# Three queues for the edge transfers, and a second staging buffer in the sort, in a graph kernel

## The chip, the cores and the metric

The kernel runs on one core of a Trainium2 chip. The metric is the device time of one execution in microseconds. Three executions of the kernel before took 7155.8, 7169.51 and 7184.21 us (median 7169.51). A fourth was profiled and took 7184.49 us, of which 7182.9 us are the span from its first to its last instruction.

## The reference

There are 3125 nodes with 64 features and 100,000 edges, given as `src` and `dst`, sorted by `dst`. Four graph networks follow one another; behind each the result is added to `x` and normalised.

1. Five layers, each of
```
h = leaky(x @ W1 + b1) @ W2 + b2
e = leaky(edge_attr_32 @ We1 + be1) @ We2 + be2
x = layernorm(x + res_w * segment_sum(h[src] * e * dot_scale, dst)) * ln_g + ln_b
```
2. A graph convolution with weights by degree.
3. Two transformer convolutions, with a softmax over the edges of each node.
4. `x + (x + segment_sum(relu(x[src] + edge_attr_64), dst))`, then the last normalisation.

Only 1 and 4 read edge attributes edge by edge. In 2 and 3 the kernel uses a matrix of edge counts between all pairs of nodes.

## The kernel before, in words

The five engines run programs of their own that are tied by semaphores. The stages are separated by barriers.

**Sort.** The edges are put into a new order, by blocks of 256 source nodes and 128 target nodes. They are laid out as 125 partitions by 800 columns, and one step (`t`, `j`) treats 8 columns, 1000 edges; there are 100 steps. SyncE loads, broadcast to all partitions, the keys and the block numbers of the step's edges (`load_keys`, lines 614 to 618, two steps ahead) and its 32-wide attributes (`load_attr`, three steps ahead). VectorE compares the keys (`find_slots`, from line 1579) to find the place of each edge. TensorE computes `e` for the five layers, which depends on nothing in the layers, and ScalarE copies it from PSUM into `stage`, a ring of four slots whose rows hold 64 floats of `edge_attr_64`, 5 x 64 floats of `e`, and 2 ids. The 64-wide attributes are loaded into the slot by a DMA that ScalarE issues (`load_stage`, line 900), behind a wait on `rows_sent`: the slot has to be free of the rows of four steps ago. GpSimd waits for that load (`stage_loaded`, line 788) and for ScalarE's last copy (`stage_ready`), and sends the rows to their places in HBM with eight indirect DMAs a step (line 792). When ScalarE's copies of the last step are done, VectorE computes tables (from line 1605), and the barrier follows.

**Unpack.** 144 groups of 8 tiles of 128 edges. For each group 8 small DMAs load the ids (`load_ids`, line 550), TensorE and VectorE count, and one-hot matrices are stored to HBM (`ohsD`).

**Edge passes.** One for each of the five layers and one for network 4. A pass has 72 pairs of groups. For a pair, SyncE loads its one-hot matrices (`load_hots`, line 688) and all three DMA-issuing engines load its 16 tiles of edge rows (`load_edges`, line 548), each engine the share of every 8 tiles that line 456 gives it. They may start on pair i when VectorE has made the messages of pair i-4 (`m_ready`). Once in four pairs an engine first reads the addresses of its tiles into registers (`starts`, line 539). ScalarE besides makes four copies of table slices a pair (`slice_tables`, line 1004). TensorE gathers the rows of pair i (line 1287, 96 matmuls) between the scatters of pair i-3 (line 1296, 48 matmuls). VectorE runs four operations a pair: the message (line 1790, in the last pass 1792), the two subtractions that split it into three bf16 parts (1804, 1810), and the one-hot of the targets (1682).

**Between** the fifth and the sixth pass lie network 2 and the two convolutions of 3, which the change doesn't touch.

Of the kernel before, what the change touches and what calls it, by code (L numbers as in the profile page):

```python
# [17 lines left out]
U16 = mybir.dt.uint16  # L18
# [6 lines left out]
D = 64  # L25
# [7 lines left out]
EP = 125  # L33
ET = E // EP
# [18 lines left out]
JB = 4  # L53
IB = ET // JB
CC = 20
NCHUNK = IB // CC
CS = 8
SR = 4
# [9 lines left out]
KEYS = [(a, min(a + P, ET)) for a in range(0, ET, P)]  # L68
# [31 lines left out]
def graph_kernel(nc, x_in, src_in, dst_in, a32_in, a64_in, w1_in, b1_in, w2_in, b2_in, we1_in, be1_in,  # L100
                 we2_in, be2_in, resw_in, dots_in, lng_in, lnb_in, gw_in, gb_in, conv_in, out):
    with ExitStack() as ctx:
# [3 lines left out]
        def sem(name):  # L106
            return ctx.enter_context(nc.semaphore(name))

        def dram(name, shape, dt=F32):
            return nc.dram_tensor(name, shape, dt, kind="Internal").ap()  # L110


        rows = dram("rows", (ROWS, ROW))
        keyT = dram("keyT", (ET, EP))
        blkT = dram("blkT", (ET, EP), BF16)
        ohsD = dram("ohsD", (NG, P, 2 * GT * P), U8)
        maskD = dram("maskD", (W, P, NP))
# [31 lines left out]
        def carver(at=0):  # L149

            at = [at]

            def carve(*shape, dt=F32):
                n = 1
                for s in shape:
                    n *= s
                words = -(-n * {F32: 4, I32: 4, U32: 4, BF16: 2, U16: 2, U8: 1}[dt] // 4)
                v = big[:, at[0]:at[0] + words]
                at[0] += words
                assert at[0] <= BIG, (at[0], BIG)  # L160
                if dt != F32:
                    v = v.bitcast(dt)
                if len(shape) == 2:
                    v = v.rearrange("p (a b) -> p a b", a=shape[0])
                if len(shape) == 3:
                    v = v.rearrange("p (a b c) -> p a b c", a=shape[0], b=shape[1])
                return v
            carve.at = at
            return carve


        carve = carver()
# [20 lines left out]
        ohv = [carve(JB * CC, 32, dt=BF16) for _ in range(2)]  # L193
        ohw = [carve(JB * CC, W + 1, dt=BF16) for _ in range(2)]
        carve = carver(shared)
        keyb = carve(2, CS * EP)
        blkb = carve(2, CS * EP, dt=BF16)
        lhot = carve(2, CS * EP + 4, dt=BF16)
        tabh = carve(IB + 1, 2, W, dt=BF16)
        keyS = carve(len(KEYS), EP)  # L200
        blkS = carve(len(KEYS), EP + 1, dt=BF16)
        stage = carve(SR, CS, ROW)
        attr = carve(SR, CS, DA)
        sidx = carve(SR, CS, dt=U32)
        late = carve.at[0]
        slotf = carve(ET)
# [42 lines left out]
        carve = carver(b_base)  # L249
# [17 lines left out]
        carve = carver()  # L267
# [19 lines left out]
        carve = carver(c_base)  # L287
# [8 lines left out]
        carve = carver(c_base)  # L296
# [19 lines left out]
        def bank(b, n=1):  # L316
            return ps[:, b * 512:(b + n) * 512]

        pacc = bank(0, 4)
        pA, pB, pC, pD = bank(4), bank(5), bank(6), bank(7)  # L320
# [13 lines left out]
        key_kept = sem("key_kept")  # L334
        key_stored = sem("key_stored")
# [8 lines left out]
        ranked = sem("ranked")  # L344
        slot_ready = sem("slot_ready")
        slot_chain = sem("slot_chain")
        stage_loaded = [sem(f"stage_loaded{r}") for r in range(SR)]
        attr_loaded = [sem(f"attr_loaded{r}") for r in range(SR)]
        edge_weights = sem("edge_weights")
        be2_chain = sem("be2_chain")  # L350
        be2_ready = sem("be2_ready")
        attr_turned = sem("attr_turned")
        attr_kept = sem("attr_kept")
        e_up = sem("e_up")
        e_biased = sem("e_biased")
        e_act = sem("e_act")
# [96 lines left out]

        PE, DVE, SP = mybir.EngineType.PE, mybir.EngineType.DVE, mybir.EngineType.SP
        POOL, SCALAR = mybir.EngineType.Pool, mybir.EngineType.Activation
        SP_SHARE, POOL_SHARE, ACT_SHARE = (0, 4), (4, 7), (7, 8)
        SOFT = 16 * (POOL_SHARE[1] - POOL_SHARE[0])
        HARD = 16 * GT - SOFT
        CLAMPED = "the table was clamped when it was made on the chip"
# [1 line left out]
        def hold(eng):  # L461

            eng.nop(nofuse=True)
# [64 lines left out]
        def past(i, k):  # L528

            return not isinstance(i, int) or i >= k  # L530

        def chunk(t, j, k):

            return t + (j + k) // JB, (j + k) % JB
# [47 lines left out]
        def _(sp):  # L582
            sp.dma_start(src_i[0:EP, :], src_in.rearrange("(p t) -> p t", p=EP)).then_inc(ids_loaded, 16)
            sp.dma_start(dst_i[0:EP, :], dst_in.rearrange("(p t) -> p t", p=EP)).then_inc(ids_loaded, 16)
            a32_v = a32_in.rearrange("(p t) f -> p t f", p=EP)

            def load_attr(t, j):
                tiles = bass.ds(j * IB + t * CS, CS)
                sp.dma_start(attr[0:EP, j, :, :], a32_v[:, tiles, :]).then_inc(attr_loaded[j], 16)
# [14 lines left out]
            sp.dma_start(be2r[0:3, :], be2_in.rearrange("(o l) f -> o (l f)", o=1).to_broadcast([3, LAYERS * D])).then_inc(edge_weights, 16)  # L604
            for k, (a, b) in enumerate(KEYS):
                sp.wait_ge(key_kept, 2 * k + 2)
                sp.dma_start(keyT[a:b, :], keyS[0:b - a, k, :]).then_inc(key_stored, 16)
                sp.dma_start(blkT[a:b, :], blkS[0:b - a, k, 0:EP]).then_inc(key_stored, 16)
            sp.wait_ge(key_stored, 32 * len(KEYS))
            sp.wait_ge(counted, NCHUNK)  # L610
# [3 lines left out]
            def load_keys(t, j):  # L614
                r = j % 2
                own = bass.ds(j * QT + t, 1)
                sp.dma_start(keyb[0:EP, r, :], keyT_v[own, :].to_broadcast([EP, CS * EP])).then_inc(key_loaded[r], 16)
                sp.dma_start(blkb[:, r, :], blkT_v[own, :].to_broadcast([P, CS * EP])).then_inc(key_loaded[r], 16)

            load_keys(0, 0)  # L620
            load_keys(0, 1)

            def feed(t, j):
                i = t * JB + j
                if not past(i, QN - 2):
                    sp.wait_ge(ranked, i + 1)
                    hold(sp)
                    load_keys(*chunk(t, j, 2))
                if past(i, 1) and not past(i, QN - 3):
                    sp.wait_ge(attr_kept, i)  # L630
                    hold(sp)
                    load_attr(*chunk(t, j, 3))

            def feed_more(t, j):
                i = t * JB + j
                sp.wait_ge(ranked, i + 1)
                hold(sp)
                load_keys(*chunk(t, j, 2))
                sp.wait_ge(attr_kept, i)
                hold(sp)  # L640
                load_attr(*chunk(t, j, 3))

            for j in range(JB):
                feed(0, j)
# [117 lines left out]
        def _(pool):  # L762
# [22 lines left out]

            with pool.Fori(0, QT) as t:
                for j in range(JB):
                    pool.wait_ge(stage_loaded[j], t * 16 + 16)
                    pool.wait_ge(stage_ready, t * JB + (j + 1))
                    hold(pool)  # L790
                    for c in range(CS):
                        pool.indirect_dma_start(  # L792
                            out=rows[:, :], out_offset=bass.IndirectOffsetOnAxis(ap=sidx[0:EP, j, c:c + 1], axis=0),
                            in_=stage[0:EP, j, c, :], in_offset=None).then_inc(rows_sent[j], 16)
# [67 lines left out]
        def _(act):  # L862
            for k, (a, b) in enumerate(KEYS):
                act.wait_ge(key_turned, 2 * k + 1)
                act.copy(keyS[0:b - a, k, :], pC[0:b - a, 0:EP]).then_inc(key_kept, 1)
                act.wait_ge(key_turned, 2 * k + 2)
                act.copy(blkS[0:b - a, k, 0:EP], pD[0:b - a, 0:EP]).then_inc(key_kept, 1)
            for s in range(NCHUNK):
# [6 lines left out]
            def bias(t, j, p):  # L875
                at = (t * JB + j) * 3 + p
                n = P if p < 2 else D
                act.wait_ge(e_up, at + 1)
                if past(at, 2):
                    act.wait_ge(e_act, at - 1)  # L880
                act.activation(hb[0:n, (j + p) % 2, :, :], ups[0:n, :, 0:2 * EP], ACT.Identity, bias=be1[0:n, p:p + 1]).then_inc(e_biased, 1)  # L881
# [10 lines left out]
            def stage_ids(t, j):  # L892
                tiles = bass.ds(j * IB + t * CS, CS)
                act.wait_ge(slot_ready, t * JB + (j + 1))
                act.copy(sidx[0:EP, j, :], slotf[0:EP, tiles])
                act.copy(stage[0:EP, j, :, IDS:ROW], ids[0:EP, tiles, :]).then_inc(stage_ready, 1)

            a64_v = a64_in.rearrange("(p t) f -> p t f", p=EP)

            def load_stage(t, j):  # L900
                act.dma_start(stage[0:EP, j, :, 0:D], a64_v[:, bass.ds(j * IB + t * CS, CS), :]).then_inc(stage_loaded[j], 16)

            def keep_attr(t, j):
                i = t * JB + j
# [5 lines left out]
            def fill(t, j, last_one=False):  # L910
                i = t * JB + j
                bias(t, j, 0)
                if past(i, 1):
                    keep_edges(*chunk(t, j, -1), 4)
                    stage_ids(*chunk(t, j, -1))
                bias(t, j, 1)
                if past(i, JB):
                    act.wait_ge(rows_sent[j], t * (16 * CS))
                    hold(act)
                load_stage(t, j)  # L920
                keep_edges(t, j, 0)
                keep_edges(t, j, 1)
                bias(t, j, 2)
                if not last_one:
                    keep_attr(*chunk(t, j, 1))
                keep_edges(t, j, 2)
                keep_edges(t, j, 3)

            keep_attr(0, 0)
            for j in range(JB):  # L930
                fill(0, j)
# [1086 lines left out]
```

## Time and profile before

| | us |
|---|---|
| profiled execution | 7184.49 |
| its span | 7182.9 |
| set-up and counting, to the first row sent | 136.4 |
| sort, from there to the barrier | 1406.7 |
| unpack | about 897 |
| five layers | about 2496 |
| networks 2 and 3 | about 1823 |
| last pass and output | about 423 |

TensorE is busy 79% of the span, VectorE 68%, GpSimd 38%, ScalarE 37%. An average over stages with different limits says little about any of them; the views by window, and what ended each engine's idle time, have to be read stage by stage. DMA instructions that SyncE and ScalarE issue count as no busy time of an engine. They stand in the timeline with a q behind the engine's name.

### The profile page before, as it was taken

What the parts mean: (1) busy time and instruction counts of PE and PEld (TensorE: products, weight loads), DVE (VectorE), ACT (ScalarE), POOL (GpSimd) and SP (SyncE); (2) the same over time, 40 slices, a digit from 0 to 9 for tenths busy, and PEclk for the clock granted to TensorE, in tenths of its full rate; (3) what the DMA queues carried; (4) which work ended last, traced back from release to release, by engine and by line L of the source; (5) the groups of instructions that cost most, each with busy time, mean ns of one, the idle gap of its engine ahead of it and who ended that gap; (6) DMA issues with size and microseconds to landing.
All of it is one profiled execution on the core that took longest, in us unless ns stands there. A gap on an engine that the chain in (4) does not pass through costs nothing. (4 is left out here: it accounts for less than half of the span.)

```text
span 7182.9 us, 255993 instructions
## 1 busy us (share of the span) xinstructions
PE 5688.4 (79%) x87510; PEld 4758.0 (66%) x87511; DVE 4863.4 (68%) x10450; ACT 2678.6 (37%) x5126; POOL 2758.3 (38%) x4136
## 2 busy tenths in 40 slices
PE   4888888846666488788787887887979998999787
PEld 3666666624444288688687786886957776777687
DVE  7555555588888677677677676777755554555688
ACT  2444444424444432222222322323643332333443
POOL 1777777853333155355354453551000000000254
PEclk9999998965656599799798897997779998999999
DMA  2677766622222467476475575664531111111376
GB/s 71 199 197 198 199 198 194 199 69 47 47 47 47 161 168 175 117 176 174 116 175 144 146 175 127 166 173 124 197 121 65 58 63 48 59 62 65 89 192 155
DMA packets 1265072, 933.90 MB, mean 130 GB/s; under 512 B 1003190, under 2 KB 1033581, under 8 KB 1255227
## 3 DMA queue, kind: packets, MB, share of 16 engines
q1 hardware_dynamic: 794406, 635.39, 29.8%
q0 software_dynamic: 224768, 240.90, 13.9%
q10 hardware_dynamic: 245652, 54.13, 3.9%
q8 instruction: 180, 2.95, 0.2%
q14 instruction: 66, 0.53, 0.0%
HBM read 673.72 MB, written 255.19 MB: 129 GB/s over the span
## 5 line engine op out<-in xcount | busy, mean ns | idle before, releaser
L548 POOL DMA_DIRECT2D big<-rows x2592 | 1385.8, 535 | 3287.8 <-issue 2140.5
L1287 PE MATMUL ps<-big 128*128 128x64 bf16 x41472 | 2073.8, 198 | 438.8 <-DMA big<-ohsD 235.2
L1287 PEld LDWEIGHTS ps<-big 128*128 128x128 fp8e4 x41472 | 1793.8, 102 | 482.4 <-issue 478.7
L1296 PE MATMUL ps<-big 128*128 128x64 bf16 x20736 | 1866.7, 203 | 28.0 <-issue 26.9
L1296 PEld LDWEIGHTS ps<-big 128*128 128x128 bf16 x20736 | 1270.5, 118 | 41.1 <-issue 33.7
L1004 ACT COPY big<-big 128x384 bf16 x1728 | 754.9, 508 | 1453.9 <-DVE big L1790 1383.7
L792 POOL DMA_INDIRECT rows<-big x800 | 1066.7, 1333 | 438.7 <-issue 365.2
L1790 DVE TENSOR_TENSOR big<-ps,big 128x1024 f32<-128x1024 f32 x360 | 440.6, 1224 | 514.2 <-PE ps L1287 514.1
L1577 DVE SCALAR_TENSOR_TENSOR big<-big 128x1000 f32<-128x1000 f32 (+1 forms) x300 | 361.9, 1206 | 573.8 <-ACT big L881 554.8
L1254 PE MATMUL ps<-identb,big 128*128 128x128 bf16 x2304 | 435.0, 288 | 347.0 <-DVE big L1697 187.0
L1205 PEld LDWEIGHTS ps<-big 128*125 128x125 f32 (+1 forms) x4800 | 632.1, 197 | 89.8 <-issue 47.7
L1457 PE MATMUL ps<-big 128*128 128x64 f32 x5000 | 645.6, 272 | 52.4 <-ACT big L1117 51.6
L1457 PEld LDWEIGHTS ps<-big 128*128 128x128 f32 x5000 | 614.8, 194 | 82.0 <-ACT big L1117 74.3
L1929 DVE CUSTOM_DVE_ANT_0 big<-ps,big 128x512 f32<-128x512 f32 (+1 forms) x700 | 414.5, 631 | 356.7 <-PE ps L1436 356.7
L1682 DVE TENSOR_TENSOR big<-iota,big 128x2048 bf16<-128x2048 bf16 (+1 forms) x720 | 647.9, 900 | 2.2 <-POOL big L810 2.2
L1205 PE MATMUL ps<-big 128*125 128x128 f32 (+1 forms) x4800 | 645.5, 283 | 0.0
L1254 PEld LDWEIGHTS ps<-identb,big 128*128 128x128 bf16 x2304 | 277.5, 130 | 516.4 <-ACT big L950 283.4
L1713 DVE TENSOR_TENSOR big<-big,ps 128x256 f32 x1152 | 479.9, 417 | 119.6 <-DVE big L1713 78.8
L950 ACT ACTIVATE big<-ps 128x512 fp8e4<-128x512 f32 x576 | 338.2, 593 | 555.4 <-PE ps L1255 530.2
L1804 DVE TENSOR_TENSOR big<-big 128x1024 f32<-128x1024 f32 x432 | 526.4, 1219 | 0.0
L1810 DVE TENSOR_TENSOR big<-big 128x1024 f32<-128x1024 f32 x432 | 525.1, 1215 | 0.2
L1117 ACT COPY big<-ps 128x512 f32<-128x512 f32 (+1 forms) x350 | 188.0, 537 | 833.4 <-PE ps L1446 833.4
(260 smaller groups left out, 7850.1 us busy)
## 6 DMA issues: line engine op xcount, KB each, us to landing
big<-ohsD SPq DMA_DIRECT2D x432, 512.0 KB, 3.8
big<-rows SPq DMA_DIRECT2D x3456, 32.0 KB, 2.7
big<-rows POOLq DMA_DIRECT2D x2592, 32.0 KB, 3.0
big<-maskD SPq DMA_DIRECT2D x50, 1600.0 KB, 6.7
big<-keyT SPq DMA_DIRECT2D x100, 488.3 KB
maskD<-big SPq DMA_DIRECT2D x25, 1600.0 KB, 6.2
ohsD<-big SPq DMA_DIRECT2D x144, 256.0 KB, 2.0
big<-rows ACTq DMA_DIRECT2D x864, 32.0 KB, 2.6
```

Of the source, the lines that this page charges most:

```text
L548: eng.dma_start(edge[:, u.r * 2 + k, j, :], rows[bass.ds(at, P), col]).then_inc(landed[u.r], 16)
L792: pool.indirect_dma_start(out=rows[:, :], out_offset=bass.IndirectOffsetOnAxis(ap=sidx[0:EP, j, c:c + 1], axis=0), in_=stage[0:EP, j, c, : ...
L1004: last = act.copy(slices[:, 2 * u.r + k // 2, k % 2, :], flat(tabq)[:, bass.ds(names[u.r * 4 + k], 6 * D)])
L1205: last = pe.matmul(to[:, a * n:(a + 1) * n], hid[0:n, (j + p) % 2, c, k * EP:(k + 1) * EP], we2[0:n, p, 0:n], start=False, stop=True, skip ...
L1254: pe.matmul(bank(2 * h + k)[:, j * P:(j + 1) * P], src[:, j, k * P:(k + 1) * P], identb[:, :], start=True, stop=True)
L1287: last = pe.matmul(pG[g % 4][:, j * D:(j + 1) * D], ohsR[:, g, at:at + P].bitcast(F8), slices[:, g, q, (3 * half + c) * D:(3 * half + c + ...
L1296: last = pe.matmul(pacc[:, bass.ds(at, D)], own[:, j % QUAD, :], upper_half(part(u, c)[:, f:f + D]), start=False, stop=False, skip_group_c ...
L1457: last = pe.matmul(bank(6 + h)[:, 0:D], pt[:, tau % 4, i * P:(i + 1) * P], vN[:, v, h * D:(h + 1) * D], start=(v == 0), stop=(v == W - 1))
L1682: return dve.tensor_tensor(to.rearrange("p (q d j) -> p q d j", q=n, j=QUAD), iota4[:, 0:P, :].unsqueeze(1).to_broadcast([P, n, P, QUAD]), ...
L1713: dve.tensor_tensor(own, own, bank(4 + m // 2)[:, m % 2 * 2 * P:(m % 2 + 1) * 2 * P], ALU.add).then_inc(c_added[m], 1)
L1804: dve.tensor_tensor(part(u, 1), part(u, 0), upper_half(part(u, 0)), ALU.subtract).then_inc(res_ready, 1)
L1810: dve.tensor_tensor(part(g, 2), part(g, 1), upper_half(part(g, 1)), ALU.subtract).then_inc(lo_ready, 1)
```

## The change

Line 456 gives each engine its share of every 8 tiles: SyncE had 4, GpSimd 3, ScalarE 1; now they have 3, 3 and 2. It holds for `load_ids` in the unpack stage and for `load_edges` in the six passes.

In the sort the 64-wide attributes go into a buffer of their own, `wide` (four slots), by a DMA that SyncE issues three steps ahead, behind the keys and the 32-wide attributes. ScalarE copies them into the ring where it issued the DMA before. GpSimd's wait for the load is gone. The keys are 16-bit integers instead of 32-bit floats, in the HBM scratch and in SBUF.

```diff
-        keyT = dram("keyT", (ET, EP))
+        keyT = dram("keyT", (ET, EP), U16)
-        keyb = carve(2, CS * EP)
+        keyb = carve(2, CS * EP, dt=U16)
-        keyS = carve(len(KEYS), EP)
+        keyS = carve(len(KEYS), EP + 1, dt=U16)
+        wide = carve(SR, CS, D)
-        SP_SHARE, POOL_SHARE, ACT_SHARE = (0, 4), (4, 7), (7, 8)
+        SP_SHARE, POOL_SHARE, ACT_SHARE = (0, 3), (3, 6), (6, 8)
 # SyncE
+            def load_wide(t, j):
+                sp.dma_start(wide[0:EP, j, :, :], a64_v[:, bass.ds(j * IB + t * CS, CS), :]).then_inc(wide_loaded[j], 16)
+            for j in range(JB):
+                load_wide(0, j)
...
                     load_attr(*chunk(t, j, 3))
+                    sp.wait_ge(wide_placed, i)
+                    hold(sp)
+                    load_wide(*chunk(t, j, 3))
 # GpSimd
-                    pool.wait_ge(stage_loaded[j], t * 16 + 16)
                     pool.wait_ge(stage_ready, t * JB + (j + 1))
 # ScalarE
-            def load_stage(t, j):
-                act.dma_start(stage[0:EP, j, :, 0:D], a64_v[...]).then_inc(stage_loaded[j], 16)
+            def place_wide(t, j):
+                act.wait_ge(wide_loaded[j], t * 16 + 16)
+                hold(act)
+                act.copy(stage[0:EP, j, :, 0:D], wide[0:EP, j, :, :]).then_inc(wide_placed, 1)
...
                     act.wait_ge(rows_sent[j], t * (16 * CS))
                     hold(act)
-                load_stage(t, j)
+                place_wide(t, j)
```

## Rows read from the trace of the kernel before

**Rows 1.** Busy time by window: length; engines; granted clock, DMA share, GB/s
```profile
200.00:1400.00 1200.00, 1023.10 (x8371) 779.56 (x8370) 683.09 (x3259) 574.79 (x973) 929.00 (x703) 0.91 0.70 198
1600.00:2400.00 800.00, 501.14 (x3316) 338.14 (x3314) 685.99 (x1936) 357.66 (x1143) 262.42 (x670) 0.60 0.21 47
2517.40:2934.90 417.50, 351.72 (x10126) 344.00 (x10122) 326.89 (x284) 119.25 (x272) 218.14 (x408) 0.93 0.69 171
6764.50:7151.20 386.70, 337.49 (x10123) 330.39 (x10119) 325.98 (x283) 190.58 (x347) 218.14 (x408) 0.97 0.74 186
6820.00:7090.00 270.00, 234.85 (x7012) 230.18 (x7010) 226.69 (x197) 134.03 (x246) 158.72 (x297) 0.96 0.77 192
```

**Rows 2.** Timeline of SyncE's queue in the first pass, four pairs: start, length
```profile
2645.22 0.39 SPq L688 DMA_DIRECT2D big<-ohsD  x1
2645.85 4.36 SPq L548 DMA_DIRECT2D big<-rows  x8
...
2669.24 0.39 SPq L688 DMA_DIRECT2D big<-ohsD  x1
```

**Rows 3.** Timeline of VectorE, four messages in the same stretch
```profile
2660.31 1.23 DVE L1790 TENSOR_TENSOR big<-ps,big 128x1024 f32<-128x1024 f32 x1 [0.24 <-PE ps L1287]
2665.18 1.23 DVE L1790 TENSOR_TENSOR big<-ps,big 128x1024 f32<-128x1024 f32 x1 [0.24 <-PE ps L1287]
2670.39 1.23 DVE L1790 TENSOR_TENSOR big<-ps,big 128x1024 f32<-128x1024 f32 x1 [0.58 <-PE ps L1287]
2679.56 1.23 DVE L1790 TENSOR_TENSOR big<-ps,big 128x1024 f32<-128x1024 f32 x1 [4.54 <-PE ps L1287]
```

**Rows 4.** Waits of the first pass (2500 to 2900 us): total, times, longest
```profile
PE ps L1287 <- DMA big<-ohsD: 39.5, 23, 3.9
```

**Rows 5.** Address loads into registers and row loads, by line: min/median/max ns
```profile
L539 SPq TENSOR_LOAD <-offs x33: 1231/1245/1259, 1614.3 to 2355.1; - x33
L539 SPq TENSOR_LOAD <-offs x12: 1862/1867/1882, 2619.0 to 2883.1; - x12
L548 ACTq DMA_DIRECT2D big<-rows x864: 337/340/1336, 2505.3 to 7139.5; - x173
```

**Rows 6.** Timeline of SyncE's queue and VectorE in the last pass
```profile
6906.67 0.38 SPq L688 DMA_DIRECT2D big<-ohsD  x1
6907.24 3.95 SPq L548 DMA_DIRECT2D big<-rows  x8
...
6928.60 0.39 SPq L688 DMA_DIRECT2D big<-ohsD  x1
6921.00 1.23 DVE L1792 TENSOR_TENSOR big<-ps,big 128x1024 f32<-128x1024 f32 x1 [0.56 <-PE ps L1287]
6925.79 1.22 DVE L1792 TENSOR_TENSOR big<-ps,big 128x1024 f32<-128x1024 f32 x1 [0.16 <-PE ps L1287]
```

**Rows 7.** Timeline of TensorE early in a pass
```profile
3535.12 0.28 PE L1296 MATMUL ps<-big 128*128 128x64 bf16 x3 [2.08 <-issue]
```

**Rows 8.** Waits of the sort (120 to 1515 us): total, times, longest
```profile
POOL rows L792 <- DMA big<-in_edge_attr: 70.8, 32, 7.8
```

**Rows 9.** Groups by line, sort from 200 to 1400 us: busy, mean ns, idle before
```profile
L792 POOL DMA_INDIRECT rows<-big x703 | 929.2, 1322 | 271.1 <-issue 206.0 <-DMA big<-in_edge_attr 62.4 <-ACT big L896 2.7
L888 ACT COPY big<-ps 125x512 f32<-125x512 f32 x354 | 205.8, 589 | 466.1 <-PE ps L1205 247.9 <-issue 218.1
```

**Rows 10.** Timeline of the sort, one of GpSimd's gaps, with ScalarE's load
```profile
674.60 0.27 ACTq L901 DMA_DIRECT2D big<-in_edge_attr  x1
684.61 0.21 ACT L896 COPY big<-big 125x16 f32 x1
702.08 1.19 POOL L792 DMA_INDIRECT rows<-big  x1 [5.02 <-DMA big<-in_edge_attr]
```

**Rows 11.** Busy time by window while only 125-partition loads run
```profile
4.00:6.00 2.00, 0.00 (x0) 0.00 (x0) 0.00 (x0) 0.00 (x0) 1.41 (x6) 1.00 0.32 131
```

**Rows 12.** Timeline, the end of the sort
```profile
1543.10 16.82 POOL L799 MEMSET big<- 128x20064 f32 x1 [32.14 <-DVEq L451]
```

More of the change, by code:

```diff
@@ L346, in graph_kernel @@
         slot_chain = sem("slot_chain")
-        stage_loaded = [sem(f"stage_loaded{r}") for r in range(SR)]
+        wide_loaded = [sem(f"wide_loaded{r}") for r in range(SR)]
         attr_loaded = [sem(f"attr_loaded{r}") for r in range(SR)]
@@ L353, in graph_kernel @@
         attr_kept = sem("attr_kept")
+        wide_placed = sem("wide_placed")
         e_up = sem("e_up")
@@ L584, in _ @@
             sp.dma_start(dst_i[0:EP, :], dst_in.rearrange("(p t) -> p t", p=EP)).then_inc(ids_loaded, 16)
+            a64_v = a64_in.rearrange("(p t) f -> p t f", p=EP)
             a32_v = a32_in.rearrange("(p t) f -> p t f", p=EP)
@@ L606, in _ @@
                 sp.wait_ge(key_kept, 2 * k + 2)
-                sp.dma_start(keyT[a:b, :], keyS[0:b - a, k, :]).then_inc(key_stored, 16)
+                sp.dma_start(keyT[a:b, :], keyS[0:b - a, k, 0:EP]).then_inc(key_stored, 16)
                 sp.dma_start(blkT[a:b, :], blkS[0:b - a, k, 0:EP]).then_inc(key_stored, 16)
@@ L641, in feed_more @@
                 load_attr(*chunk(t, j, 3))
+                sp.wait_ge(wide_placed, i)
+                hold(sp)
+                load_wide(*chunk(t, j, 3))
             for j in range(JB):
@@ L864, in _ @@
                 act.wait_ge(key_turned, 2 * k + 1)
-                act.copy(keyS[0:b - a, k, :], pC[0:b - a, 0:EP]).then_inc(key_kept, 1)
+                act.copy(keyS[0:b - a, k, 0:EP], pC[0:b - a, 0:EP]).then_inc(key_kept, 1)
                 act.wait_ge(key_turned, 2 * k + 2)
@@ L896, in stage_ids @@
                 act.copy(stage[0:EP, j, :, IDS:ROW], ids[0:EP, tiles, :]).then_inc(stage_ready, 1)
-            a64_v = a64_in.rearrange("(p t) f -> p t f", p=EP)
-            def load_stage(t, j):
-                act.dma_start(stage[0:EP, j, :, 0:D], a64_v[:, bass.ds(j * IB + t * CS, CS), :]).then_inc(stage_loaded[j], 16)
+            def place_wide(t, j):
+                act.wait_ge(wide_loaded[j], t * 16 + 16)
+                hold(act)
+                act.copy(stage[0:EP, j, :, 0:D], wide[0:EP, j, :, :]).then_inc(wide_placed, 1)
             def keep_attr(t, j):
```

## The prediction

> **What bounds the kernel now.** I read the busy times by window first, to part the stages, then in each stage the waits, then the timeline of the engine that the waits point at.
>
> In the passes over the edges the windows show that TensorE and VectorE are both short of full [rows 1]: 417.5 us go by between the first and the last message of a pass of 72 pairs, so 71 steps of 5.88 us. Of VectorE's operations a pair has four of 1.22 us. The waits name TensorE waiting for the one-hot matrices, which SyncE loads [rows 4]. SyncE's queue shows why. From one load of a one-hot to that of four pairs later there are 2669.24 - 2645.22 = 24.02 us, 6.0 a pair, and inside them SyncE issues without a pause: eight row loads follow each other at (4.36 - 0.34) / 7 = 0.574 us (0.34 being the last one's own length) [rows 2]. One gap between pairs in four is longer by the register load of the addresses, 1.87 us [rows 5]. So SyncE's issuing sets the pace. TensorE and VectorE run at their own pace until they have used up the lead, and then stand still: messages start 4.87 us and 5.21 us apart, and then 9.17 with 4.54 us idle [rows 3]. The last pass is the same thing at (6928.60 - 6906.67) / 4 = 5.48 us [rows 6], beside the 386.7 / 71 = 5.45 us that a pair takes [rows 1].
>
> In the sort the windows show GpSimd the fullest beside TensorE, and a steady DMA rate of 198 GB/s [rows 1]. A step takes 1200 / (703 / 8) = 13.66 us. GpSimd needs 8 x (1.322 + 0.306) = 13.0 of them, 0.306 being its usual gap (206.0 / 672) [rows 9]. What is left are waits for the load that ScalarE issues: 70.8 us in 32 waits, of which the usual gap takes 32 x 0.3 = 9.6, so 61 us [rows 8]. One of them in full: the rows were ready at 684.8, the load issued at 674.6, and GpSimd got on at 702.1 [rows 10]. The load took 27 us to land. Where that comes from can be estimated. While only loads of 125 partitions run, the mean share of the 16 DMA engines is 0.32, at 131 GB/s [rows 11]. That is 5 engines of 16, at 26.2 GB/s each. A step's broadcast keys (500,000 B), 32-wide (128,000 B) and 64-wide attributes (256,000 B) then cost each of the five 3.8 + 1.0 + 2.0 = 6.8 us. All together are busy 0.70 x 16 x 13.66 = 153 us a step; less 5 x 6.8 the rest is (153 - 34) / 16 = 7.4 us on each. So the five have some 14.2 us of work in a step of 13.7: they are full, and what is queued on them lands late.
>
> The Trainium skill (DMA: Bandwidth & Descriptors, section on why a DMA increments its semaphore by 16) says that a hardware-generated DMA uses the largest number of engines up to 16 that divides the slowest dimension, which is 5 for 125 partitions; the trace agrees with 0.32 [rows 11].
>
> **Row loads 4/3/1 to 3/3/2.** SyncE issues 6 instead of 8 row loads a pair. For four pairs it saves 8 x 0.574 = 4.59 us. It also loads 24 instead of 32 addresses: 16 cost 1.245 and 32 cost 1.867 us [rows 5], so 8 fewer save 0.31. That gives 24.02 - 4.90 = 19.12, 4.78 us a pair. What is late next is TensorE with VectorE behind it, and their pace is seen between the stalls: 4.87, sometimes 5.21, of which the catching up after a stall gives some back; I take 4.88. A pass takes 71 x 4.88 = 346 us. At the start of a pass TensorE also has waits of up to 2 us that no load explains [rows 7]. I leave 9 us a pass for them (estimate): 355. Before: 417.5. The gain is 62 us, five times: 310.
>
> In the last pass SyncE saves 8 x (3.95 - 0.34) / 7 = 4.13 and 0.31 of 21.93: 17.5, 4.37 a pair. Messages start 4.79 apart where nothing stalls [rows 6]. 71 x 4.79 + 5 = 345 instead of 386.7: 42.
>
> ScalarE gets the two loads a pair. They cost it two issues of 0.34 us and the same few register instructions as on SyncE, about 1 us. It is busy 119 of 417 us [rows 1], so there is room: hidden. Without that cover it would be 1 us a pair, 427 us in all, so ScalarE's issue time is the cost to watch (a rival below). GpSimd keeps three tiles. In the unpack stage the same line moves one small load a group from SyncE to ScalarE, about 0.5 us in 144 groups. VectorE sets the pace there (686 of 800 us busy), and ScalarE is idle half of the time (358) [rows 1]. I take 0, with +10 and, were ScalarE the limit, +70 as the far end.
>
> The same page has a rule against this part (section Issuing engines are not separate DMA queues): all queues end on the same 16 engines, and issuing from several saves only the sequencer's time, which is usually small beside the transfer. By the rule the part is worth about nothing. Here the sequencer's time is the bound by the rows [rows 2], so I hold to the rows; the case in which the rule is right is a rival.
>
> **Sort, the load moved and the keys halved.** The load leaves GpSimd's path. It is issued three steps ahead, some 39 us, against a landing of 27 us. The keys take 250,000 B less, 1.9 us less on each of the five engines: 12.3 us of work in a step that GpSimd will pace at 13.0. So the queues should shorten too. SyncE's added wait, on ScalarE's copy one step ago, stands behind its wait for VectorE's ranks of this step, which come later; behind it only the next keys are queued. Its price is 0; were the 64-wide load late, ScalarE would stand with all its copies behind it, and the step would stay at 13.7. ScalarE's new copy of 125 x 512 costs about 0.59 us, like the copies from PSUM of that size [rows 9]; it stands behind the wait for the slot, and GpSimd has at least ten us of rows ready then (684.8 against 702.08 - 5.02 = 697.1, where its last DMA ended) [rows 10]: 0. The 16-bit keys leave VectorE's comparison two-operand with one fp32 operand; I take its time unchanged.
>
> GpSimd's gaps go: 61 us. The stage's end hangs not on GpSimd, which has been idle for 32 us when the barrier opens [rows 12], but on ScalarE's last copy and VectorE's tables behind it. ScalarE is held by the ring, four steps behind GpSimd, so it gains nearly the same. I take 55, with 0 and 61 as ends.
>
> **The sum.** 310 + 42 + 55 = 407. From 7184.5 that leaves 6777. The profiled execution lies 15 us above the median shown, so I forecast 6765.
>
> **Rivals.**
> 1. *The DMA engines become the bound of the passes.* They are busy 0.69 x 5.88 = 4.1 us a pair now [rows 1]; at 4.88 us this is a share of 0.84, and 0.87 in the last pass. If 0.77, the highest share that a long window shows, is what they can give, a pair takes 4.1 / 0.77 = 5.34 us in the layers and the last pass stays at 5.45. Gain: 71 x 0.54 x 5 - 10 + 0 + 55, about 235: 6935. For it: both passes are full of 32 KB loads in short rows. Against: the 0.77 was itself set by SyncE's pace, and between stalls the pace is 4.87 already.
> 2. *The sort gains nothing*, since the five engines stay full or ScalarE now waits for the load as GpSimd did: 6765 + 55 = 6820.
> 3. *SyncE's issuing only looks like the bound*, and the transfers or the waits behind them set it: only the sort gains, 7115. Against: 6.0 us a pair, twice, equals the pace in both kinds of passes.
> 4. *Slower: ScalarE becomes the issuer that sets the pace.* Its four copies take 4 x 0.51 less overlap, some 1.8 us; four loads add 4 x (x + 0.13). At the longest issue seen, 1.34 us [rows 5], that makes 7.7 us a pair, 1.8 more than now, over 426 steps 760 us, less the sort: 7870. It decides from x = 0.9 us on, where the pair is back at 5.88. Against: the median is 0.34.
>
> **How the numbers follow.** Forecast 0.50, rival 2 0.20 (it lies in the range), rival 1 0.20, rival 3 0.06, rival 4 0.03, and 0.01 for no change. Low end: no stumbling at the start of the passes (5 x 9 + 5) and 61 in the sort leave 6765 - 56, and some pairs go at VectorE's four operations alone: 6700. High end: rival 1, 6935. Faster by over 0.5% (36 us, about what can be told from no change here) 0.96, within it 0.01, slower 0.03.
>
> **What would show it.** In a pass, the loads of one-hots on SyncE's queue less than 5 us apart with pauses between, TensorE's wait for ohsD near zero, messages 4.9 us apart throughout, the pass about 355 us, the clock near 1.0 and the DMA share near 0.84. In the sort, GpSimd waiting only its 0.3 us between DMAs, a step at 13.0 us, the DMA rate near 189 GB/s. If the messages lie 5.2 us apart or more with SyncE's issues stretched, rival 1 holds; if ScalarE's issues last near 1 us, rival 4.

## The result and the profile after

The changed kernel takes 6842.2 us (median of 4 runs, 6824.5 to 6859.2) where the kernel before took 7176.9 in runs beside it (7155.8 to 7187.9). The ratio is 0.9537, with an interval of 0.9502 to 0.9572: faster, by 335 us. The forecast was 6765 in a range of 6700 to 6935.

Both profiled executions, cut into stages (us). A stage in the passes runs from the first message to the last, as in the prediction; "starts" are the stretches from one pass's last message to the next one's first.

| stage | before | after | difference |
|---|---|---|---|
| sort, first row sent to barrier | 1406.7 | 1336.0 | -71 |
| barrier to first message | 974.3 | 980.3 | +6 |
| five layer passes, sum | 2084.3 | 1813.6 | -271 |
| four starts between them, sum | 312.7 | 333.9 | +21 |
| fifth pass to last pass | 1850.0 | 1859.5 | +9.5 |
| last pass | 386.8 | 355.1 | -32 |
| rest | 31.7 | 31.7 | 0 |

The sum is -337, the difference of the spans (7182.9 and 6846.2). The stretch between the fifth and the last pass came out between 1820 and 1889 us in the runs below, so its +9.5 says little.

The first view of the changed kernel is the busy time by window, to be laid beside [rows 1]: length; PE, PEld, DVE, ACT, POOL; granted clock, DMA share, GB/s.

```profile
200.00:1400.00 1200.00, 1073.44 (x8782) 813.59 (x8780) 719.22 (x3426) 644.58 (x1114) 974.78 (x740) 0.95 0.65 187
1530.00:2330.00 800.00, 499.49 (x3312) 335.91 (x3312) 685.84 (x1934) 355.69 (x1143) 261.90 (x668) 0.60 0.21 47
2520.00:2780.00 260.00, 240.70 (x7438) 235.84 (x7434) 237.73 (x208) 90.78 (x208) 165.57 (x310) 1.00 0.93 209
6520.00:6790.00 270.00, 252.28 (x7848) 247.39 (x7845) 249.69 (x217) 146.75 (x269) 174.03 (x327) 1.00 0.93 211
```

GpSimd sends 740 row sets in the 1200 us where it sent 703, so a sort step takes 1200 / (740 / 8) = 12.97 us. The unpack stage (second row) stands still. In the passes TensorE and VectorE are over 0.91 busy, the granted clock is 1.00 where it was 0.93 and 0.97, and the DMA engines are at 0.93, where 0.77 was the highest in a window of [rows 1]. The higher clock isn't what the shorter passes need as an explanation: before, the first step behind a stall was 4.87 us already [rows 3], and the steps without a stop are 4.5 to 4.9 us now.

SyncE's queue in the first pass, four pairs, beside [rows 2]: start, length.

```profile
2600.64 0.38 SPq L703 DMA_DIRECT2D big<-ohsD  x1
2601.26 3.16 SPq L550 DMA_DIRECT2D big<-rows  x6
...
2605.07 0.38 SPq L703 DMA_DIRECT2D big<-ohsD  x1
2609.86 0.38 SPq L703 DMA_DIRECT2D big<-ohsD  x1
2614.40 0.38 SPq L703 DMA_DIRECT2D big<-ohsD  x1
2620.68 0.38 SPq L703 DMA_DIRECT2D big<-ohsD  x1
```

From one-hot load to one-hot load four pairs on there are 20.04 us where there were 24.02, and SyncE now has pauses. The one wait that it shows is for VectorE's messages (this and the next row are waits: total us, times, longest; of SyncE from 2520 to 2800 us, and of TensorE from 2520 to 2780). For TensorE no wait for ohsD is left [rows 4].

```profile
SPq L465 <- DVE big L1804: 20.3, 42, 0.8
...
PE ps L1301 <- issue: 15.8, 25, 1.1
```

VectorE's messages in the same pairs, beside [rows 3], and TensorE's one stop between them:

```profile
2598.82 1.23 DVE L1804 TENSOR_TENSOR big<-ps,big 128x1024 f32<-128x1024 f32 x1 [1.29 <-PE ps L1301]
2603.62 1.23 DVE L1804 TENSOR_TENSOR big<-ps,big 128x1024 f32<-128x1024 f32 x1 [0.17 <-PE ps L1301]
2608.42 1.23 DVE L1804 TENSOR_TENSOR big<-ps,big 128x1024 f32<-128x1024 f32 x1 [0.17 <-PE ps L1301]
2612.96 1.22 DVE L1804 TENSOR_TENSOR big<-ps,big 128x1024 f32<-128x1024 f32 x1
2618.89 1.23 DVE L1804 TENSOR_TENSOR big<-ps,big 128x1024 f32<-128x1024 f32 x1 [1.31 <-PE ps L1301]
...
2613.89 0.34 PE L1301 MATMUL ps<-big 128*128 128x64 bf16 x6 [1.03 <-issue]
```

The messages come 4.8, 4.8, 4.5 and 5.9 us apart, this pattern again and again. Between the 9th and the 69th message the mean step is 5.04 us in each of the five layer passes (4.97 in the last pass); the stretch shown has 5.01. The 9.17 of [rows 3] is gone. The long one stands behind TensorE's 1.03 us at the turn of its loop, once in four pairs ("issue": it waits for nothing that the profile shows). There it loads into registers where a pair's scatters go; for the other three pairs that load stands between the two halves of the pair before. The next message comes late by it, with VectorE idle for 1.31 us.

What the loads take from issue to landing has grown (page, part 6; the row loads took 2.7, 3.0 and 2.6 us before, the one-hots 3.8):

```profile
big<-ohsD SPq DMA_DIRECT2D x432, 512.0 KB, 4.1
big<-rows POOLq DMA_DIRECT2D x2592, 32.0 KB, 4.1
big<-rows SPq DMA_DIRECT2D x2592, 32.0 KB, 4.0
...
big<-rows ACTq DMA_DIRECT2D x1728, 32.0 KB, 3.9
```

In the sort the waits (120 to 1515 us) have lost the row of [rows 8]. GpSimd is left with its usual gap in 799 of 800 cases, and it is ScalarE that waits, for a slot of the ring to be sent:

```profile
POOL rows L806 <- issue: 374.2, 800, 130.7
ACT big L915 <- DMA rows<-big: 205.6, 61, 7.6
```

At the start of the first pass something is longer than before. First the kernel before, then the changed one, ScalarE and TensorE, each with the idle time before it:

```profile
2505.28 4.16 ACTq L548 DMA_DIRECT2D big<-rows  x8
2510.63 6.70 ACT L1004 COPY big<-big 128x384 bf16 x16 [8.08 <-issue]
...
2512.52 7.64 PE L1287 MATMUL ps<-big 128*128 128x64 bf16 x193 [13.50 <-ACT big L1004]
```

```profile
2436.47 8.52 ACTq L550 DMA_DIRECT2D big<-rows  x16
2446.18 6.29 ACT L1018 COPY big<-big 128x384 bf16 x15 [12.92 <-issue]
...
2448.07 4.09 PE L1301 MATMUL ps<-big 128*128 128x64 bf16 x86 [18.34 <-ACT big L1018]
```

ScalarE issues its first row loads ahead of the copies that cut the tables into slices. There are 16 now instead of 8, the copies come 4.8 us later, and TensorE, whose first gathers need the slices, stands for 18.34 us instead of 13.50.

### The profile page after: what moved, and what is told of

Its sections match the earlier page's. It is cut to its first block and busy times, and to the rows that moved or that the text cites. A ratio compares the mean times of both kernels' runs of the same rounds, so it can differ in the third digit from the quotient of the medians.

```text
span 6846.2 us, 256189 instructions
## 1 busy us (share of the span) xinstructions
PE 5573.9 (81%) x87504; PEld 4638.5 (68%) x87511; DVE 4858.8 (71%) x10450; ACT 2721.8 (40%) x5226; POOL 2756.1 (40%) x4136
## 3 DMA queue, kind: packets, MB, share of 16 engines
q8 instruction: 180, 2.95, 0.2%
## 5 line engine op out<-in xcount | busy, mean ns | idle before, releaser
L1301 PE MATMUL ps<-big 128*128 128x64 bf16 x41472 | 1961.9, 194 | 275.8 <-ACT big L1018 124.9
L1301 PEld LDWEIGHTS ps<-big 128*128 128x128 fp8e4 x41472 | 1714.2, 99 | 316.1 <-issue 315.1
L1310 PE MATMUL ps<-big 128*128 128x64 bf16 x20736 | 1820.0, 199 | 32.3 <-issue 31.3
L1310 PEld LDWEIGHTS ps<-big 128*128 128x128 bf16 x20736 | 1238.9, 116 | 46.8 <-issue 37.8
```

The source lines that it names most:

```text
L1301: last = pe.matmul(pG[g % 4][:, j * D:(j + 1) * D], ohsR[:, g, at:at + P].bitcast(F8), slices[:, g, q, (3 * half + c) * D:(3 * half + c + ...
L1310: last = pe.matmul(pacc[:, bass.ds(at, D)], own[:, j % QUAD, :], upper_half(part(u, c)[:, f:f + D]), start=False, stop=False, skip_group_c ...
```

## The experiments

The runs part the change in three questions: which part gives what, why the sort's load landed late, and what holds the passes at 5.04 us a pair. The expectations are quoted as they were written. Ratios are against the kernel before, run on the same chip.

**The shares alone.** The kernel before with

```
-        SP_SHARE, POOL_SHARE, ACT_SHARE = (0, 4), (4, 7), (7, 8)
+        SP_SHARE, POOL_SHARE, ACT_SHARE = (0, 3), (3, 6), (6, 8)
```

> The kernel before with the shares 3/3/2 alone. Theory A (SyncE's issuing was the bound of the passes, and ScalarE's longer first issue costs about 5 us at each pass start): the passes take 361 to 365 us from first to last message as in the changed kernel, TensorE's wait ahead of a layer's first gather is 18.3 us instead of 13.5, the sort stays at 1407 us from its first row to the barrier; in all about 265 us less than before, 6910. Rival (the passes gained from something in the sort part, such as rows lying otherwise): the passes stay near 417 us. If ScalarE's starts cost nothing: 6880.

Measured: 6912.0 us, ratio 0.9626 (0.9596 to 0.9656). Passes 363.5, 361.8, 361.0, 364.6, 361.6 and 354.9; starts 82.4 to 84.0; sort 1413.6, with GpSimd still waiting 75.7 us for its load, 26 times. So the whole gain of the passes, and the whole loss at their starts, comes from this line. SyncE's issuing was the bound. (The sort is 7 us longer here than in the trace of the kernel before, though nothing in it was changed: so much can lie between two traces of the same stage.)

**The sort alone.** The changed kernel with that line put back.

> The changed kernel with the shares 4/3/1 of before: the sort's two edits alone. Theory A: the sort takes 1336 us from its first row to the barrier instead of 1407, the passes stay at 417 us and their starts at 13.5 us of TensorE waiting; 71 us less in all, 7106. Rival: the two parts work together (the sort's gain needs ScalarE or SyncE otherwise loaded), then the sort lies elsewhere than at 1336.

Measured: 7101.9, ratio 0.9897 (0.9864 to 0.993). Sort 1339.3, passes 411.5 to 414.6 and 385.0. The two parts add up: 0.9626 x 0.9897 = 0.9527, beside 0.9537. (The layer passes are some 4 us shorter than the 416 to 417 of the kernel before, though their line wasn't changed; the three runs that follow have it too. SyncE's queue goes with it: in this run eight row loads take 4.29 us where they took 4.36, and four pairs 23.7 instead of 24.02. Why an issue was shorter there stays open.)

**Why the load landed late.** Three edits, each alone. The first halves the keys' bytes and leaves the load of the 64-wide attributes where it was (kernel before):

```
-        keyT = dram("keyT", (ET, EP))
+        keyT = dram("keyT", (ET, EP), U16)
-        keyb = carve(2, CS * EP)
+        keyb = carve(2, CS * EP, dt=U16)
...
-        keyS = carve(len(KEYS), EP)
+        keyS = carve(len(KEYS), EP + 1, dt=U16)
```

> The kernel before with the 16-bit keys alone; ScalarE still issues the 64-wide load and GpSimd waits for it. Theory B (the five DMA engines that carry the 125-partition loads were full, and 1.9 us less for each in a step makes the loads land early): GpSimd's wait for the load falls from 61 us to under 15, the sort takes 1340 to 1355 us. Theory C (what counts is that GpSimd's path has no load of a 27 us landing in it any more): the sort stays near 1400 us, and the wait near 61 us.

The second keeps 32-bit keys and moves the load only (the changed kernel with the lines above undone, the old shares, and an SBUF area enlarged from 46464 to 48576 words to hold it):

> The kernel before with the second staging buffer alone: SyncE loads the 64-wide attributes three steps ahead, ScalarE copies them, the keys stay 32-bit (the large SBUF tensor is made longer, or it would not fit). Theory B: the five engines stay full with 14.2 us of work a step, so the step stays near 13.6 us; the wait turns up elsewhere (ScalarE on the 64-wide load or on the slot), the sort takes 1390 to 1410 us. Theory C: GpSimd has no wait left and the sort takes 1336 to 1345 us.

The third keeps the bytes a partition gets, but the broadcast goes to 128 partitions instead of 125 (kernel before):

```
-                sp.dma_start(keyb[0:EP, r, :], keyT_v[own, :].to_broadcast([EP, CS * EP])).then_inc(key_loaded[r], 16)
+                sp.dma_start(keyb[:, r, :], keyT_v[own, :].to_broadcast([P, CS * EP])).then_inc(key_loaded[r], 16)
```

> The kernel before, except that the 32-bit keys are broadcast to 128 partitions instead of 125 (three more that nothing reads). Theory B (a load of 125 partitions runs on 5 of the 16 DMA engines): spread over 16 engines the keys cost each 1.2 us a step instead of 3.8 on five, the five are no longer full, GpSimd's wait for the load is gone and the sort takes 1336 to 1350 us, with no byte less. Rival (what the DMAs carry in all is the bound, 198 GB/s): 2% more bytes, so the sort stays at 1407 or grows.

Measured, in this order: sort 1336.8, 1334.4 and 1337.1 us; one time each, 7093, 7087 and 7108. Their windows of the sort (the same columns as above):

```profile
200.00:1400.00 1200.00, 1083.19 (x8791) 816.66 (x8783) 717.99 (x3431) 592.92 (x1024) 974.85 (x739) 0.95 0.69 187
```

```profile
200.00:1400.00 1200.00, 1078.77 (x8792) 816.78 (x8791) 719.12 (x3436) 643.23 (x1117) 974.09 (x742) 0.95 0.69 206
```

```profile
200.00:1400.00 1200.00, 1084.42 (x8791) 819.24 (x8791) 717.87 (x3430) 594.47 (x1024) 974.90 (x739) 0.95 0.77 207
```

All three give the whole 70 us, and GpSimd sends 739 to 742 row sets in the window as in the changed kernel. The third row settles the cause, since its edit takes no byte away and moves no load: it adds 12,000 B a step and only spreads the keys over more engines. GpSimd's wait for the load that ScalarE issues, 70.8 us in 32 waits before [rows 8], is down to

```profile
POOL rows L792 <- DMA big<-in_edge_attr: 0.9, 3, 0.3
```

The rate is 207 GB/s at a share of 0.77 (higher than before for the most part because the step is shorter), and the load is in time. So it wasn't the total rate of 198 GB/s [rows 1]. What is left is the prediction's estimate that five engines were full; no view shows a single engine's share, so their fullness itself is worked out and not seen. The first row is the same cause met by fewer bytes. The second shows that the cover also does it, with 32-bit keys and 206 GB/s: my expectation that the step would stay at 13.6 us fell. Each edit is enough, and the second one done beside the first gives nothing more, since GpSimd's own 8 x (1.319 + 0.306) = 13.0 us a step is the floor.

**Are the DMA engines what holds the passes at 5.04?** The share of 0.93 and the longer landings spoke for it. The changed kernel, with only the first half of each one-hot matrix loaded from the fifth pair of a pass on (the gathers then read in the other half what the first four pairs left there):

```
+                half = slice(0, (2 if u.known else 1) * GT * P)
+                sp.dma_start(ohsR[:, 2 * u.r:2 * u.r + 2, half], ohsD[bass.ds(u.i * 2, 2)].rearrange("g p f -> p g f")[:, :, half]).then_inc(ohs_loaded[u.r], 16)
```

> The changed kernel, where from the fifth pair of a pass on only the first half of each one-hot matrix is loaded (what is gathered is wrong), with as many DMAs: 256 KB less of about 1 MB a pair. Rival F (the DMA engines set the pace of the passes): the mean pair falls clearly below 5.04, at most to TensorE's 4.87. Theory E: the DMA share falls from 0.93 to about 0.7, the pairs keep their pattern of 4.9, 4.9, 4.5 and 5.9 us, the passes stay at 361 to 363 us.

```profile
2520.00:2780.00 260.00, 241.80 (x7481) 237.16 (x7479) 237.87 (x208) 91.25 (x208) 166.18 (x310) 1.00 0.69 156
```

The share falls from 0.93 to 0.69, the row loads land in 2.7 us again, and the passes take 359.0, 362.3, 359.9, 359.0, 362.2 and 353.1: nothing gained beyond 1%. The mean step, from the 9th to the 69th message of the first pass, is 5.03 us beside 5.04. Not the DMA engines.

**Is it TensorE's own work?** The changed kernel, with two of the three bf16 parts of each message scattered (the third is left out of the sums):

```
-                for c in range(3):
+                for c in range(2):
```

> The changed kernel with two of the three bf16 parts scattered (32 instead of 48 scatter matmuls a pair; the third part is left out of the sums). Theory E (TensorE's own work and its turn of the loop set the pace): a pair gets shorter, to the 4.6 to 4.8 us of VectorE and SyncE, a pass takes 335 to 350 us. Rival (SyncE's issuing is still what sets 5.04): the passes stay at 361 to 365 us.

```profile
2520.00:2780.00 260.00, 235.83 (x7266) 230.72 (x7263) 259.00 (x228) 98.27 (x224) 180.09 (x337) 1.00 0.98 224
```

6673.5 us in one run, passes of 330.1 to 331.6 and 323.0, a little below the range expected. A third of the scatters gone takes the pair to 4.6 us, and now VectorE is busy for 259.0 of 260 us, at 1.14 us an operation, four a pair: it is the next bound, just behind. The DMA engines go along to a share of 0.98. SyncE is as near:

```profile
2601.74 0.38 SPq L703 DMA_DIRECT2D big<-ohsD  x1
...
2620.50 0.38 SPq L703 DMA_DIRECT2D big<-ohsD  x1
```

Four pairs take it 18.76 us, and it shows no wait in this stretch, so this is its own pace: 4.69 a pair, a little slower than VectorE, paid out of the lead that it has from the start of the pass. Near the end of the pass some steps are 5.0 to 5.2 us again. Both bounds lie below the 5.04 of the changed kernel. In the changed kernel TensorE is the bound: 240.7 us busy and 15.8 waiting on "issue" leave 3.5 of 260.

**Halving the loop turns.** The changed kernel, with TensorE's loop over eight pairs instead of four, so that it turns half as often:

```
...
+                with pe.Fori(0, (PT - 2) // 2) as t:
+                    for i in range(2 * PR):
+                        body(Pair(t * 2 + (2 + i // PR), i % PR), i == 0, i == 2 * PR - 1)
...
```

> The changed kernel, with TensorE's loop over the pairs unrolled to eight pairs a turn instead of four, and the addresses of the next pair loaded in the middle of each pair but the last of a turn. Theory E (every fourth pair takes 5.9 us instead of 4.87 because TensorE's queue jumps back and then reads its addresses, 1.0 us idle): every eighth pair is long, the mean pair goes from 5.04 to 4.95 and the passes to about 356 us, 35 to 40 us less in all, 6805. Rival F (the DMA engines, at a share of 0.93, set 5.04): the pairs share the time otherwise, the passes stay at 362 us.

Measured: 7675.6, ratio 1.0686 (1.0647 to 1.0725); passes of 486 to 502. The expectation was far off. The rows are the page's instruction queue (packets, MB, share; 180 packets and 2.95 MB in the changed kernel) and TensorE's waits from 2600 to 2900 us:

```profile
q8 instruction: 702, 11.50, 0.6%
...
PE ps L1301 <- issue: 81.3, 57, 9.1
```

There are (41472 + 20736) / 432 = 144 matmuls and as many weight loads in a pair, so at least 1152 instructions in the loop of four pairs and 2304 in that of eight. The kernel with the loop of eight fetches 522 packets more, of (11.50 - 2.95) / 522 = 16.4 KB. The loop turns 8 times in each of six passes, so that is nearly 11 packets a turn (an estimate, since the longer code around the loop takes a few of them): the loop is fetched anew on every turn, and TensorE stands for up to 9.1 us on "issue". With the stops its granted clock falls to 0.87 from 2600 to 2900 us, and it is busy 5.4 us a pair instead of 4.6.

The Trainium skill (Runtime: NRT & Kernel Launch, section Instruction fetch mechanics) says that TensorE's instruction memory holds 2048 instructions and is refilled in blocks of 256. It also says that a taken branch to a block outside the current window of two blocks has to wait for the fetch. The runs agree with the size: 1152 instructions stay, 2304 don't. They don't agree with a window of two blocks, since the loop of four pairs jumps back over more than four blocks, 16 times in each of six passes, and the whole changed kernel fetches 180 packets, as many as the kernel before. What the loop turn itself costs the run with the loop of eight could not show. The link from the 1.03 us to the turn stands on the timeline alone: it comes every fourth pair.

**The starts of the passes.** Three runs. The first puts ScalarE's first loads behind its slice copies (`load_edges` for the first four pairs is taken out from ahead of the loop and done in it):

```
-                for r in range(PR):
-                    load_edges(act, v, Pair(0, r), *ACT_SHARE, col, edge_loaded)
...
-                        if u.live(PR):
-                            load_edges(act, v, u, *ACT_SHARE, col, edge_loaded)
+                        load_edges(act, v, u, *ACT_SHARE, col, edge_loaded)
```

> The changed kernel, except that ScalarE issues its row loads of a pass's first four pairs behind the table slices of each pair instead of ahead of them all. Theory D (at a pass start TensorE waits for slices that stand behind 16 loads and a register load on ScalarE, 18.3 us): TensorE's wait falls to about 9 us and each of the six passes starts 9 us earlier, 55 us in all, 6787. Rival (the wait ahead of the first gather is set by the tables or by SyncE's loads): nothing changes, 6842.

The second gives ScalarE still more ahead of the slices:

```
-        SP_SHARE, POOL_SHARE, ACT_SHARE = (0, 3), (3, 6), (6, 8)
+        SP_SHARE, POOL_SHARE, ACT_SHARE = (0, 2), (2, 5), (5, 8)
```

> The changed kernel with shares 2/3/3: one more of 8 loads from SyncE to ScalarE. Theory (SyncE is no longer the bound, and each load of ScalarE at a pass start costs 0.5 us): the passes stay at 361 to 365 us, TensorE waits 23 us ahead of a layer's first gather instead of 18.3, about 27 us more in all. If SyncE's issuing still counted: the passes get shorter.

Measured: starts of 74.2 to 74.7 us in the first (the changed kernel: 82.3 to 84.1) and of 88.3 to 89.2 in the second, with the passes as they were in both. In the second SyncE issues two of every 8 row loads instead of three, and the mean step of the first pass stays at 5.04: its issuing no longer sets the pace. The second, from the timeline of ScalarE and TensorE:

```profile
2444.13 12.87 ACTq L550 DMA_DIRECT2D big<-rows  x24
2458.17 6.70 ACT L1018 COPY big<-big 128x384 bf16 x16 [17.73 <-issue]
...
2460.06 5.17 PE L1301 MATMUL ps<-big 128*128 128x64 bf16 x94 [23.16 <-ACT big L1018]
```

Issues of 8, 16 and 24 loads take 4.16, 8.52 and 12.87 us, and TensorE stands for 13.50, 18.34 and 23.16. Each load that ScalarE issues there costs the path (23.16 - 13.50) / 16 = 0.60 us. In the first run the wait is 9.56. The second's time is 6906 in one run, the first's 6827.6 (ratio 0.9522, 0.9482 to 0.9562), which the intervals don't part from the changed kernel: of the 55 us expected the profiled execution shows 45, the medians 15.

The third also moves ScalarE's register loads of addresses from the pass to the start of the layer, where it is idle. It ran beside the changed kernel on one chip.

> The changed kernel once more, to set the next one against it on the same chip: 6842 us, ratio 0.953 to the kernel before.

> The changed kernel, with ScalarE's first row loads behind the slices as in the run before, and its two register loads (addresses and tables of the first four pairs) at the start of the layer instead of between the tables and the slices. Theory D: TensorE's wait ahead of a layer's first gather falls from 18.3 us (9.6 with the loads moved alone) to about 7, six times; about 70 us less than the changed kernel, 6775. Rival: the time saved at the start is lost in the first pairs, whose rows now come later, and the whole stays within 20 us of the changed kernel.

Measured: 6843.3 for the changed kernel (ratio 0.9551, 0.9527 to 0.9574) and 6788.9 for the third (0.9469, 0.9446 to 0.9492). The intervals lie apart: 54 us (70 were expected), 0.8% less, the fastest version found that leaves nothing out. Its starts take 71.6 to 71.9 us, and TensorE stands for 7.45:

```profile
2439.47 9.32 PE L1301 MATMUL ps<-big 128*128 128x64 bf16 x240 [7.45 <-ACT big L1018]
```

## Why the prediction was right, and where it was short

The mechanism was right in each part, and rivals 1 to 4 fell. For the profiled execution the working gave 6777, and it took 6847.8: 71 us more. By terms:

- **Layer passes, 310 forecast, 271 measured.** The failed size is the pair: 4.88 forecast, 5.04 measured, which is 5 x 71 x 0.156 = 55 us. I read the next pace from the three steps between the stalls. The fourth, the one with the stall of 9.17 in [rows 3], by this reading hid a stop that isn't SyncE's: TensorE's at the turn of its loop, 1.03 us now. None of the three steps beside it had a stop on "issue" of over 0.24 us in that stretch, and now every fourth step has it, 0.26 us a pair. That is more than the 0.16 missing; the other three steps, at 4.80, 4.80 and 4.54, went faster than I took them. The 9 us left for the start were 4 too many: 362.7 (the mean pass) - 71 x 5.036 = 5, which gives 19 us back. The last 3 us are that the five passes before took 2084.3 and not five times the first.
- **Last pass, 42 forecast, 32 measured.** The same term: 4.97 a pair, and 4.79 forecast.
- **SyncE's own pace, 19.12 us for four pairs forecast.** It is 18.76 where it never waits, in the run without the third part. Nothing in the sum hangs on it.
- **What is late next.** TensorE with VectorE just behind, as said; TensorE, not VectorE, by the run without the third part (4.6 a pair).
- **ScalarE's loads, "hidden".** True in the steady pairs, where nothing waits for ScalarE's loads now. Wrong at the six pass starts, where the same loads come in a burst ahead of the slices, and ScalarE is the engine that TensorE waits for. I weighed ScalarE's mean load of the pass (119 of 417 us) and never read its first 10 us. This is a missing term, 27 us by the first five starts (6 + 21), and by the starts of the two other orders it is caused by those loads.
- **Sort, 55 forecast, 71 measured**, above the end of 61 that I gave as the most. All of GpSimd's waits went (61). I had let ScalarE's hold by the ring take a bit back; instead the barrier came sooner by 10 us more than that gain. GpSimd's idle time before it fell from 32.14 [rows 12] to 28.16:

```profile
1472.24 16.82 POOL L813 MEMSET big<- 128x20064 f32 x1 [28.16 <-DVEq L453]
```

  That is 4 us of the 10, though the other runs with this sort have 28.2 to 30.5 there. Over 100 steps the step of 12.97 instead of the 13.0 worked out is 3 more; the rest wasn't pursued.
- **Sort's cause.** I gave two reasons, the cover of three steps and the five emptier engines, as if both were needed. Each is enough alone.
- **Unpack, 0**: as the second window shows, right.

With the +9.5 between the fifth and the last pass, which can't be told from nothing, this makes 39 + 10 + 27 - 16 + 9.5 = 70 of the 71 us.

Rival 1 deserves a word, since half of its signs came: a DMA share of 0.93 (0.84 forecast) and landings half as long again. The 4.1 us of work a pair in the prediction are a little low, because the window from the first to the last message leaves out loads that were issued ahead of it: from 2600 to 2860 us the share was 0.70 at 6.0 us a pair, 4.2. It became 0.93 x 5.04 = 4.7, for the same bytes (175 GB/s x 6.0 us and 209 x 5.01 both make 1.05 MB a pair). So a packet takes some 11% longer now that they follow closer. But halving the one-hots' bytes moved no pass, and less TensorE work moved all of them, at a still higher share. A high share here showed a pace set elsewhere.

The rule of the Trainium skill against this part (DMA: Bandwidth & Descriptors, section Issuing engines are not separate DMA queues) is that several issuers save only the sequencer's time, usually small beside the transfer. The runs bear out its words and not its "usually": the issuing was all there was to gain, a ratio of 0.9626, because each load of 32 KB cost SyncE 0.574 us [rows 2], eight times a pair.

## What to carry to other kernels

When issues are moved to an engine that has room on average, read that engine's timeline also at the places where it issues in a burst: at the start of a loop the burst stood ahead of the one operation that another engine was waiting for, and moving it behind gave back more than it had cost (starts of 74 us, where before they took 78 and the change made them 84). The whole time showed it clear of the noise only with the register loads moved too. When a stall every few steps goes, the steps between the stalls are not all the next pace: a small stop once in a loop turn that the stall used to hide stays. A late DMA is not proof that all 16 engines are full: look at how many partitions the transfers beside it have, before shrinking them.

## What was not expected of the hardware, and what stays open

- TensorE's loop of 2304 instructions is fetched on each turn (702 packets in the kernel instead of 180), and a pair takes about 7 us instead of 5.04. The loop of 1152 isn't fetched again.
- The DMA engines ran at a mean share of 0.98 and 224 GB/s over 260 us, and VectorE, which set the pace there, waited 1.0 us in all; TensorE waited for one-hots four times, 4.4 us, which did not show in that pace.
- An issue of a row load is 0.34 us long on ScalarE; in a burst of 8, 16 or 24 they follow each other at 0.54 us.
- With the keys broadcast to 125 partitions another load landed after 27 us in the gap of [rows 10], and GpSimd waited 70.8 us for such loads; with the same broadcast to 128 partitions it waited 0.9.

Not tried: carrying TensorE's address loads over the loop turn, which would test the 1.03 us; a shorter issue of GpSimd's row sets, which is the floor of the sort now; what makes the pairs stumble at the start of a pass; and a view of the five DMA engines by themselves.
